# Moving the output stores of a conditioned residual kernel from SyncE's queue to ScalarE's

## The reference, cut to what matters

```python
x = x + einsum('bct,bcd->bdt', x, L0_cond_weights[itok_B_1_198])      # 200 matrices of 128 x 128
x = x + einsum('bct,bcd->bdt', x, L1_cond_weights[itok_B_0_7]) \
      + fside_8xS_0[itok_B_0_7][:, :, None]                           # 8 matrices, 8 biases
```

## Time and profile before

| | us |
|---|---|
| median of 3 runs | 347.73 |
| lowest, highest | 347.19, 347.92 |
| the profiled execution's own time | 348.84 |
| its span, first to last instruction | 347.1 |

### The profile page before, as it was taken

The page is one execution under the profiler, slowest core; times in us unless marked ns, Lnnn a source line. Parts: engine busy times, 40 slices in busy tenths (PEclk is TensorE's granted clock), DMA queues, the critical chain, the costliest instruction groups (busy, mean ns, idle before and its releaser), DMA issues.

```text
span 347.1 us, 5157 instructions
## 1 busy us (share of the span) xinstructions
PE 266.8 (77%) x774; PEld 129.5 (37%) x774; DVE 126.3 (36%) x202; ACT 96.9 (28%) x135; POOL 65.3 (19%) x249
## 2 busy tenths in 40 slices
PE   1799991986798896979877779777679877778980
PEld 1344450442344442434433334433334433333430
DVE  3254541333334242433433344333334333334440
ACT  1133350221333133332232232422242222323230
POOL 2400222112221112221122212122221212221000
PEclk9999997899989898998999999999999999999996
DMA  7999969999999999999999999999999999999994
GB/s 306 410 409 393 378 248 351 424 418 397 417 431 415 433 423 427 417 416 427 432 425 427 427 423 432 421 436 423 419 431 425 432 430 426 423 421 440 419 405 171
DMA packets 24058, 140.80 MB, mean 406 GB/s; under 512 B 2673, under 2 KB 14322, under 8 KB 15474
## 3 DMA queue, kind: packets, MB, share of 16 engines
q1 hardware_dynamic: 23760, 140.20, 97.9%
q10 hardware_dynamic: 290, 0.53, 0.4%
HBM read 76.03 MB, written 67.11 MB: 412 GB/s over the span
## 4 chain that ended last, share of the span: by engine, by line
DMA 56%; SPq 27%; issue 9%; PE 5%; ACT 0%
DMA out<-xy 47%; SPq L127 10%; DMA xy<-x 9%; SPq L122 7%; PE y_ps L306 5%; SPq L128 4%; SPq L142 3%; SPq L145 2%; ACT xy L402 0%; PE m_ps L287 0%; SPq L159 0%; SPq L148 0%; SPq L153 0%; SPq L163 0%; SPq L154 0%
## 5 line engine op out<-in xcount | busy, mean ns | idle before, releaser
L306 PE MATMUL y_ps<-xy,m_sb 128*128 128x512 f32 x512 | 245.5, 616 | 61.3 <-DMA xy<-x 60.3
L306 PEld LDWEIGHTS y_ps<-xy,m_sb 128*128 128x128 f32 x512 | 92.9, 196 | 164.9 <-issue 164.9
L402 ACT ACTIVATE xy<-y_ps,j_pick 128x512 f32<-128x512 f32 x128 | 87.9, 687 | 233.1 <-PE y_ps L306 233.1
L378 DVE TENSOR_SCALAR xy<-y_ps,j_pick 128x512 f32<-128x512 f32 x128 | 96.1, 751 | 156.5 <-PE y_ps L306 156.5
L238 POOL COPY w_pick<-w_home 128x128 f32 x112 | 32.8, 293 | 245.4 <-issue 245.4
L287 PEld LDWEIGHTS m_ps<-j_pick,w_pick 128*128 128x128 f32 x224 | 35.4, 199 | 28.7 <-issue 28.7
L370 DVE TENSOR_TENSOR m_sb<-m_ps,j_pick 128x256 f32<-128x256 f32 x64 | 27.1, 424 | 45.2 <-PE m_ps L287 44.6
L287 PE MATMUL m_ps<-j_pick,w_pick 128*128 128x128 f32 x224 | 35.1, 281 | 0.0
L240 POOL COPY j_pick<-j_all 128x129 f32 x112 | 33.0, 295 | 0.1
L402 ACT ACT_TABLE_LOAD x7 | 9.0, 1283 | 7.9 <-POOL j_pick L252 7.8
L287 PE MATMUL m_ps<-j_pick,w_home 128*128 128x128 f32 x32 | 5.5, 297 | 6.7 <-DMA w_home<-w_t 6.7
(11 more groups left out here) (16 smaller groups left out, 2.8 us busy)
## 6 DMA issues: line engine op xcount, KB each, us to landing
xy<-x SPq DMA_DIRECT2D x30, 2048.0 KB, 15.1
out<-xy SPq DMA_DIRECT2D x29, 2048.0 KB, 13.4
w_home<-w_t SPq DMA_DIRECT2D x128, 64.0 KB
out<-xy SPq DMA_DIRECT2D x5, 1024.0 KB, 6.8
xy<-x SPq DMA_DIRECT2D x3, 1024.0 KB, 7.8
xy<-x SPq DMA_DIRECT2D x4, 256.0 KB, 12.6
j_all<-w_bias SPq DMA_DIRECT2D x1, 516.0 KB, 3.7
out<-xy SPq DMA_DIRECT2D x2, 256.0 KB, 5.1
```

Source lines behind the costliest of these rows:

```text
L306: nc.tensor.matmul(y_ps[:, b % YB, h, :], m_sb[:, s, k, :], xy[:, s, k, half(h)], start=True, stop=True).then_inc(y_ready, 1)
L378: nc.vector.tensor_scalar(xy[:, s, k, half(0)], y_ps[:, b % YB, 0, :], j_pick[:, s, k, D:D + 1], None, ALU.add).then_inc(left_out[b % YB], 1)
L402: nc.scalar.activation(xy[:, s, k, half(1)], y_ps[:, b % YB, 1, :], ACT.Identity, bias=j_pick[:, s, k, D:D + 1]).then_inc(right_out[b % YB ...
```

## The change

SyncE no longer issues stores (but for two halves at the very end). ScalarE issues each on its own queue, right after the last eviction of the four, or, in the first two fours of round 0, of the pair. For that, round 0 is unrolled in ScalarE's stream. SyncE keeps the loads of x and w0 in their old order; each reload waits for `stored[q]` as before.

```diff
@@ SyncE
-            def wait_out(r, s): ...
-            def store_quad(r, q): ...
-            def store_pair(r, s): ...
             sp.wait_ge(home_ready, 4)
             load_w0_of(1, 0)
-            for s in range(QUAD + 1):
-                store_pair(0, s)
             load_quad_again(1, 0)
             load_w0_of(1, 1)
-            store_pair(0, QUAD + 1)
             with sp.Fori(1, ROUNDS - 1) as r:
                 for q in range(1, QUADS + 1):
                     now = (r, q) if q < QUADS else (r + 1, 0)
                     after = (r, q + 1) if q + 1 < QUADS else (r + 1, q + 1 - QUADS)
                     load_w0_of(*after)
-                    store_quad(*((r, q - AHEAD) if q >= AHEAD else (r - 1, q - AHEAD + QUADS)))
                     load_quad_again(*now)
-            for q in range(1, QUADS):
-                if q < QUADS - 1:
-                    load_w0_of(ROUNDS - 1, q + 1)
-                store_quad(*((ROUNDS - 1, q - AHEAD) if q >= AHEAD else (ROUNDS - 2, q - AHEAD + QUADS)))
-                if q < QUADS - 1:
-                    load_quad_again(ROUNDS - 1, q)
+            for q in range(1, QUADS - 1):
+                load_w0_of(ROUNDS - 1, q + 1)
+                load_quad_again(ROUNDS - 1, q)
...
-            for q in range(1, QUADS - 1):
-                store_quad(ROUNDS - 1, q)
-            store_pair(ROUNDS - 1, LAST - 1)
@@ ScalarE
+            def wait_out(r, s):
+                for k in range(PAIR):
+                    b = s * PAIR + k
+                    act.wait_ge(left_out[b % YB], r * (ROUND_B // YB) + (b // YB + 1))
+                    act.wait_ge(right_out[b % YB], r * (ROUND_B // YB) + (b // YB + 1))
+
+            def store_quad(r, q):
+
+                wait_out(r, q * QUAD + QUAD - 1)
+                act.dma_start(quad_of(out, r, q), slots(q)).then_inc(stored[q], 16)
+
+            def store_pair(r, s):
+                wait_out(r, s)
+                act.dma_start(pair_of(out, r * QUADS + s // QUAD, s), xy[:, s, :, :].rearrange("c k t -> c (k t)"))\
+                  .then_inc(stored[s // QUAD], 16)
...
-            with act.Fori(0, ROUNDS - 1) as r:
+            for s in range(RING):
+                for k in range(PAIR):
+                    right(0, s, k)
+                if s < BY_PAIR * QUAD:
+                    store_pair(0, s)
+                elif s % QUAD == QUAD - 1:
+                    store_quad(0, s // QUAD)
+            with act.Fori(1, ROUNDS - 1) as r:
                 for s in range(RING):
                     for k in range(PAIR):
                         right(r, s, k)
+                    if s % QUAD == QUAD - 1:
+                        store_quad(r, s // QUAD)
             for s in range(RING - 1):
                 for k in range(PAIR):
                     right(ROUNDS - 1, s, k)
+                if s % QUAD == QUAD - 1:
+                    store_quad(ROUNDS - 1, s // QUAD)
+            store_pair(ROUNDS - 1, LAST - 1)
```

More of the change, by code:

```diff
@@ L39, in conditioned_residual_kernel @@
     YB = 2
-    AHEAD = QUADS - 1
     BY_PAIR = 2
@@ L148, in load_pair @@
                 sp.dma_start(xy[:, s, :, :].rearrange("c k t -> c (k t)"), pair_of(x, n, s)).then_inc(loaded, 16)
[L150 to L164, removed]
             def load_quad_again(r, q):
```

## The result

The changed kernel takes 352.05 us (median of 13 runs, 347.25 to 354.95) against 348.09 us for the kernel before (13 runs, 347.19 to 349.88). The ratio is 1.0069, with a 95% interval from 1.0046 to 1.0093. This ratio leaves out executions more than 1.5% above a kernel's own fastest, four of the changed kernel's thirteen; the medians, which keep them, stand 1.1% apart. The forecast was 343.7 us, faster. The execution that was profiled, 347.25 us, is the changed kernel's fastest; it is even 1.6 us shorter than the profiled execution of the kernel before. So its rows show where time moves, not the whole of a usual run's loss.

What follows compares the result with a forecast made beforehand. The kernel was taken as bound by its transfers, all issued from SP. -4.7 us (the hole) + 0.7 us (the end) = -4.0 us, so 347.73 - 4.0 = 343.7 us; own range 342.2 to 345.2, with rivals 340.9 to 349.7.

Steps and rivals of the forecast that it cites:

- step (3): Engines empty at 44 to 48 us, early in the run: earlier stores fill this, gaining 4.7 us, between 3.1 and 6.8.
- step (2): ScalarE taking on the stores: about 0.35 us of issue each, 0.35 to 0.8 allowed, hidden by its idle time: 0 us.
- step (4): Stretch after 60 us: loads and stores in two queues, served about equally, cost 0 us; bounds 0 and 6.0.
- step (5): End of the run: last loads share engines and land later, beyond 4.4 us of cover: 0.7 us lost, bounds 0 and 5.5.
- C: Rival, chance 0.19: mixed loads and stores stretch packets through the whole middle, costing 6.0 us; slower, 349.7 us.
- B: Rival, chance 0.14: the hole fills, but the last loads lose their cover by 4 us or more; no change, about 347.4 us.
- Theory S: Named for the experiments: two queues reshuffle which DMA engine is where, and engines in step slow each other.

Runs made afterwards that it cites:

- the copy: Against the kernel before, all computing left out, only transfers kept; stores on SyncE's queue (one) 339.80 us, or on ScalarE's (two) 339.76 us.
- r0_act: Against the kernel before, only round 0's stores go to ScalarE; SyncE issues stores from round 1 on in the old order: 344.05 us, ratio 0.9898.
- all_but_r0: Against the changed kernel, round 0's stores stay on SyncE in the old order; ScalarE issues all from round 1 on: 355.69 us, ratio 1.0240.
- last_round_sp: Against the changed kernel, the last round's stores are issued by SyncE in the order of before: 350.83 us, ratio 1.0087.
- pair_stores: Against the changed kernel, every four is stored as two pairs of 1 MB: 347.96 us, ratio 0.9996.
- stores_later: Against the changed kernel, from round 1 on ScalarE issues each four's store one pair later: 352.54 us, ratio 1.0130.
- no w0: one queue, two: Kernel before (one) and changed kernel (two), each without the w0 loads of rounds 1 to 7: 327.73 us and 327.94 us.
- 8 KB loads: one queue, two: Kernel before (one) and changed kernel (two), an 8 KB load replacing each w0 load of rounds 1 to 7: 333.72 us and 337.77 us.

## Why the prediction was wrong

**The hole, step (3): the mechanism right, the size nearly.** It was put at 4.7 us between 3.1 and 6.8. Alone it is worth 347.51 - 344.05 = 3.5 us, with an interval from 0.75 to 1.29%, 2.6 to 4.5 us. The window's 6.2 us is more than the time kept: part of it is only moved. Two details were off: the reload of four 1 went out at 45.89 us, not 43.4, and TensorE's wait there fell from 7.40 to 6.51 us, not 2, since its load took until 60.2 us behind the stores.

**ScalarE's issues, step (2): right.** Its stores take 0.34 us each, and its long gaps still end with TensorE.

**The steady order, step (4): the step that failed.** It took 0 us, "if a packet lasts as long", from bounds of 0 and 6.0. Measured, what moving the stores costs from round 1 on is by the ratios 1.0069 / 0.9898 = 1.0173, 6.0 us, and by the medians 8.0. Two of its premises fell. First, "the engines serve both about equally" holds by packets and not by bytes. It came from one row of 1.4 us with 256 KB stores on both queues, where the packets are alike. In the full stretch q1 has w0 packets of 512 B among those of 16 KB, and q10 only 16 KB. Without small loads the two queues cost 0.2 us; with 8 KB ones, 4.1 us. Second, a packet doesn't last as long: the share stays at 1.01 while the rate falls from 425 to 419 GB/s. The step also priced a longer landing at nothing, because "it fits". Landings of 19.2 and 13.0 us with compute and waits do fill the 41.3 us of a round. Whether that costs time isn't shown: the copy's 41.2 us fill it as well, at the full rate.

**The end, step (5): the place right, the size open.** It took 0.7 us of 0 to 5.5 for lost cover. The cover was indeed used up: from the last issue to the end of the span there are 345.5 - 340.40 = 5.1 us, where there were 9.1. The load took 3.6 us longer (19.04 against 15.43), but it landed only 322.43 - 321.67 = 0.8 us later in the span, and TensorE's lower clock added 1.7 us, which no term had. The 3.7 us of emptiness at 330 us and the 3.6 us less behind 340 us cancel, so the profiled execution shows no loss by the end as a whole. That of a usual run wasn't traced.

**The rivals.** C had the sign and nearly the price (349.7 us; rate after 60 us under 418 GB/s, measured 412), and its packets that last longer are there. A mixture by itself doesn't do it, as the copies show. B foresaw the empty engines ahead of the last stores and a last landing of about 5 us, but not the cost in the middle.

**The page.** The Trainium skill, "DMA: Bandwidth & Descriptors", section "Queues, rings and completion order", says that an engine drains a whole packet of descriptors from one ring before it goes to the next. The trace agrees that turns go by packets: what the profile records as packets, 512 B or 16 KB, alternate one by one (274.200 and 274.224 us). How many descriptors such a packet has, no run here shows. The prediction cited this section and read "goes round" as "evenly", which is so for packets and not for bytes.

**What stays open.** How the late and uneven service turns into lost time. Two things go with the loss, in the stretch from 88 to 300 us of each profiled execution. "Extra" is the time by which packets of 8 and 16 KB lasted longer than the usual 611 ns for 16 KB, summed over them and divided by 16 engines:

| run | GB/s | granted clock | extra us |
|---|---|---|---|
| before | 425 | 0.97 | 0.8 |
| r0_act | 425 | 0.97 | 1.1 |
| after | 419 | 0.94 | 3.6 |
| all_but_r0 | 418 | 0.93 | 3.5 |
| last_round_sp | 411 | 0.93 | 5.2 |
| pair_stores | 417 | 0.90 | 4.8 |
| stores_later | 413 | 0.88 | 6.3 |
| no w0: one queue, two | 430, 427 | 1.00, 0.97 | 0.7, 2.0 |
| 8 KB loads: one queue, two | 424, 419 | 0.97, 0.93 | 0.1, 2.6 |
| copy: one queue, two | 425, 426 | nothing computes | 0.7, 0.3 |

The longer packets are the whole fall from 425 to 419 GB/s in that stretch: 3.6 - 0.8 = 2.8 us, where the rate says 3.0. They come in short bursts; the worst, from 268 to 272 us, has q1 nearly alone and 311 GB/s. The clock is the rival that no run tests: where x comes unevenly, TensorE waits longer at a time (up to 4.8 us instead of 2.7), its granted clock is lower afterwards, and the results that the stores need come later. Theory S would have it that uneven turns put engines into step. No run here separates these. Nor is there a trace of a usual execution of the changed kernel, which takes 4.8 us more than the profiled one.

## What to carry to other kernels

A second queue isn't a free place in line: look at what else stands in the first. Here the engines took turns by packets, so count a transfer's packets and not its bytes: 64 KB in rows of 512 B held up what stood behind it as long as a 2 MB store's packets lasted, and the other queue's large transfers went first. Moving an issue is worth most where the queue had run dry, and such a place can be mended alone: here moving the six stores of round 0 gives 344.05 us, faster than both kernels. And read the rate beside the busy share: at a share of 1.01 in both kernels, 425 and 419 GB/s were the only sign of the loss in the middle. A buffer's circle that adds up to the period, and a chain that runs through it, are no proof that it sets the pace; here kernels without the loss had them too.

## What wasn't expected of the hardware

The DMA engines alternated packet by packet between two queues, whatever the packets' size: 85 packets with 0.09 MB against 88 with 1.43 MB in 3.5 us. With the engines full, a new transfer's packets began 3.4 to 3.8 us after its issue in the cases above, and with them nearly empty after 0.85 us. On two queues with the same traffic, loads took 28.5 and stores 12.7 us to land, against 15.2 and 18.7 on one, at the same 425 to 426 GB/s. 112 loads of 8 KB cost 6.0 us on one queue (333.72 against 327.73), 53 ns each, where their bytes at 425 GB/s are worth 2 us. And for over 3 us near the end no more than about one DMA engine of 16 was at work (shares 0.08 and 0.06), on the rest of what the others had done with; they had nothing to do, since the next store waited for TensorE.
